# The value products of an image in two visits of two head groups instead of four visits of one

## The reference, cut to what matters

```python
q = (x @ q_w + q_b).reshape(B, N, H, hd).transpose(0, 2, 1, 3)
kv = (cond @ kv_w + kv_b).reshape(B, condN, 2, H, hd)
attn = softmax(einsum('bhnd,bhmd->bhnm', q * scale, k), axis=-1)
out  = einsum('bhnm,bhmd->bhnd', attn, v)          # the value products
x = x + out.transpose(0, 2, 1, 3).reshape(B, N, C) @ proj_w + proj_b
# then: norms, router (softmax, top 2 of 8), two expert layers with silu, weighted sum
```

## Time and profile before

| | |
|---|---|
| median of the runs | 849.52 us |
| span of the profiled execution (first to last instruction) | 811.2 us |
| of it, images in the pipeline (first to last product PV) | 47 to 491 us |
| PE busy | 710.0 us, 88% |
| DVE busy | 613.0 us, 76% |
| ACT busy | 514.1 us, 63% |
| POOL busy | 534.4 us, 66% |
| mean granted PE clock | 0.938 |

### The profile page before, as it was taken

One profiled execution on the slowest core, in us unless ns is written; L12 is line 12 of the kernel. 1 busy time (PEld: TensorE's weight loads), 2 busy tenths in 40 slices (PEclk: granted clock), 3 DMA queues, 4 the chain that ended last, 5 costly groups with the idle time before them and its releaser, 6 DMA issues.

```text
span 811.2 us, 17210 instructions
## 1 busy us (share of the span) xinstructions
PE 710.0 (88%) x5180; PEld 495.4 (61%) x5180; DVE 613.0 (76%) x2106; ACT 514.1 (63%) x1053; POOL 534.4 (66%) x756
## 2 busy tenths in 40 slices
PE   1799999999899989997999987978899999999950
PEld 0565566565565556565566655756688888887740
DVE  3666768978688878787888785677678888889962
ACT  0466666566575766565667656757587777787840
POOL 5522526777687877867688674674367777766672
PEclk9889999899898999899999998989899999999985
DMA  6454536435454455454354427556699887889955
GB/s 187 102 118 134 124 113 142 140 103 165 105 145 138 124 159 133 145 139 140 94 123 102 106 71 250 192 179 218 229 331 309 282 256 248 275 283 360 387 201 175
DMA packets 152292, 146.54 MB, mean 181 GB/s; under 512 B 53403, under 2 KB 108584, under 8 KB 152040
## 3 DMA queue, kind: packets, MB, share of 16 engines
q1 hardware_dynamic: 140808, 121.57, 50.6%
q0 software_dynamic: 9088, 19.68, 7.0%
q10 hardware_dynamic: 2304, 4.20, 1.4%
HBM read 81.56 MB, written 40.86 MB: 151 GB/s over the span
## 4 chain that ended last, share of the span: by engine, by line
PE 59%; DVE 13%; DMA 8%; ACT 6%; issue 6%; SPq 5%; POOL 4%; POOLq 0%; DVEq 0%; ACTq 0%
PE po L656 6%; PE pt L645 6%; SPq L413 5%; DMA qd<-nm 4%; PE ps L632 4%; PE pm L665 3%; PE ps L566 2%; DVE mx L1021 2%; PE ps L568 2%; PE pt L566 2%; PE pm L623 2%; PE pm L750 2%; PE pm L728 2%; PE ps L567 2%; PE pm L752 2%
## 5 line engine op out<-in xcount | busy, mean ns | idle before, releaser
L845 ACT ACTIVATE P<-pt 77x512 f32<-77x512 f32 x256 | 152.1, 595 | 107.2 <-PE pt L645 106.0
L1417 POOL DMA_INDIRECT ys<-yo,to x156 | 161.1, 1033 | 65.2 <-issue 38.9
L1410 POOL DMA_INDIRECT xs<-zz,idx x128 | 132.3, 1034 | 67.2 <-issue 28.3
L1021 DVE TENSOR_REDUCE mx<-ps 128x4 f32<-128x308 f32 x256 | 117.1, 468 | 35.6 <-PE ps L632 34.3
L1280 DVE TENSOR_TENSOR sl<-sf,sh 128x512 fp32r<-128x512 f32 x156 | 107.4, 693 | 47.7 <-ACT sh L898 33.0
L645 PE MATMUL pt<-qd,kc 128*77 128x512 f32 x256 | 115.0, 450 | 13.2 <-DMA qd<-nm 13.1
L656 PE MATMUL po<-P,v 77*9 77x128 f32 x2048 | 106.6, 282 | 0.0
L632 PE MATMUL ps<-kd,qc 128*128 128x308 f32 x256 | 100.5, 395 | 3.6 <-DVE mx L1021 3.2
L1344 POOL TENSOR_SCALAR ve<-mv 128x4 f32<-128x4 f32 x48 | 12.6, 262 | 104.6 <-DVE mv L934 103.0
L896 ACT ACTIVATE sf<-ps 128x512 f32<-128x512 f32 x78 | 46.8, 600 | 49.1 <-PE ps L568 49.1
L632 PEld LDWEIGHTS ps<-kd,qc 128*128 128x128 f32 x256 | 51.0, 200 | 26.6 <-issue 15.2
(11 more groups left out here) (234 smaller groups left out, 1924.1 us busy)
## 6 DMA issues: line engine op xcount, KB each, us to landing
qd<-qc SPq DMA_DIRECT2D x128, 128.0 KB
ws<-wsd SPq DMA_DIRECT2D x26, 512.0 KB, 4.7
w1o<-wsd SPq DMA_DIRECT2D x26, 512.0 KB
w2o<-wsd SPq DMA_DIRECT2D x26, 512.0 KB, 5.0
xb<-xs SPq DMA_DIRECT2D x39, 288.0 KB
kd<-kc SPq DMA_DIRECT2D x128, 77.0 KB, 2.3
wsd<-ws SPq DMA_DIRECT2D x8, 1024.0 KB, 4.3
y<-ys SPq DMA_DIRECT2D x32, 256.0 KB, 6.0
```

Source lines behind the costliest of these rows:

```text
L845: eng.activation(P[k % 4][:, :], pT[k % 2][0:CS, :], ACT.Exp).then_inc(sems["p"], 1)
L1021: eng.tensor_reduce(mx[b % 2][:, 4 * g:4 * g + 4], ps[k % 2][:, 0:KC].rearrange("p (j m) -> p j m", j=4), AX.X, ALU.max, negate=True).then ...
L1410: eng.indirect_dma_start(out=xs, out_offset=at, in_=zz[b][:, j % 4, :], in_offset=None).then_inc(sems[f"sw{b}"], 16)
L1417: eng.indirect_dma_start(out=ys, out_offset=at, in_=yo[u % NYO][:, q, :], in_offset=None).then_inc(sems[f"ys{u % NYO}"], 16)
```

## The change

The string `SLOTS` gets groups joined by a plus sign: Pv2 and Pv3 stand together where Pv2 stood, Pu0 and Pu1 together where Pu0 stood. A joined group counts as one slot, so `near` and `go()` see two slots fewer in each iteration. Nothing is put between the two products of a pair. The buffers of `P` get a name for their number, which stays 4. No product, copy or DMA is added or removed.

```diff
-SLOTS = "SC0 Pv2 ST0 ON SC1 Pv3 ST1 MT SC2 ST2 PR Pu0 OT SC3 ST3 Pu1"
+SLOTS = "SC0 Pv2+Pv3 ST0 ON SC1 ST1 MT SC2 ST2 PR Pu0+Pu1 OT SC3 ST3"
+NP = 4
@@ stage_order
         if t % 2 == 0 and ok(t):
-            steps.append(("QD", t // 2))
+            steps.append([("QD", t // 2)])
...
-        for s in SLOTS.split():
-            name, b = of[s[:2]]
-            if ok(b):
-                steps.append((name, b, int(s[2:])) if s[2:] else (name, b))
+        for slot in SLOTS.split():
+            group = []
+            for s in slot.split("+"):
+                name, b = of[s[:2]]
+                if ok(b):
+                    group.append((name, b, int(s[2:])) if s[2:] else (name, b))
+            if group:
+                steps.append(group)
         n = max(len(steps), 1)
         fed = 0
         for k in range(n):
             if k < len(steps):
-                put(steps[k])
+                for step in steps[k]:
+                    put(step)
@@ tiles
-        P = tile(sa, "P", [CS, 4 * S], F, 4)
+        P = tile(sa, "P", [CS, 4 * S], F, NP)
@@ tensor, PV
-                                     P[k % 4][:, j * S:(j + 1) * S], start=True, stop=True)
+                                     P[k % NP][:, j * S:(j + 1) * S], start=True, stop=True)
@@ scalar, ST
-                w.wait_ge("Og", k - 3)
-                eng.activation(P[k % 4][:, :], pT[k % 2][0:CS, :], ACT.Exp).then_inc(sems["p"], 1)
+                w.wait_ge("Og", k - NP + 1)
+                eng.activation(P[k % NP][:, :], pT[k % 2][0:CS, :], ACT.Exp).then_inc(sems["p"], 1)
```

## The result

The changed kernel takes 862.9 us (median of 4, 860.7 to 865.3) against 848.4 for the kernel before beside it: 2.1% slower, ratio 1.021 (95% interval 1.016 to 1.026). Timed twice more it gave 1.014 (1.008 to 1.021) and 1.017 (1.005 to 1.029). A ratio uses only executions within 1.5% of the fastest of their kernel and a median uses all, so the two can differ a little. The forecast was 834.5 us and faster.

What follows compares the result with a forecast made beforehand. PE's queue was taken to bound the first stage: 37 us gross less returns left 12, raised to 15 for double counting. That took the span from 811.2 to 796.2, plus 38.3 around it: 834.5 us, range 816 to 852.

Steps and rivals of the forecast that it cites:

- What bounds the kernel: First stage: PE's own queue sets the pace, with 6 to 8 us idle in each 100; DVE comes next.
- What a visit costs: Value products on PE: a lone visit costs 0.50 us, a pair 0.76; a pair saves 0.29 us.
- the rival in which a second group doesn't overlap: Pairs on PE: a merge gives only 0.17 us, 22 us gross less 22 of returns; 849 us, chance 0.05.
- Gross gain, 37 us: First stage, PE: 128 merges at 0.29 us each, at the full clock; bounds 31 and 38 us.
- Pv3's wait, 13 us in about 30 places: PE at Pv3 waits for ST3's exponential: loss 0.37 us in 30 images, 0.1 in 16; bounds 0 and 24 us.
- ACT's order, KG iterations, DVE: Returns: ACT's earlier copy of `po` 0.5 us, longer PE waits for KG's evacuation 4.5, queued DVE steps 2.
- The DMAs into `qd`, 3 us: Faster iterations leave the maxima's DMA less time to land before MT; 3 us return, bounds 0 and 11.
- The end of the stage: Fewer go() calls per iteration delay the last router's TP and scatters, so the first block starts later: 2 us, bounds 0 and 3.
- The sum of the returns, 22 us of 37: All waits and delays coming back, less 3 us counted double, leaving a 15 us gain.
- the other engines swallow it: Slack is small in several places, so waits take back the whole PE gain: about 850 us, chance 0.13.
- Slower by the clock: More waits at Pv3 lower the granted clock; doubled low time costs 22 us: 857 us, chance 0.12.
- The second stage keeps its length: Sign of a right forecast: the stage after the last value product, untouched by the change, stays equally long.

Runs made afterwards that it cites:

- second profile: The kernel before, unchanged, run and profiled once more: 848.4 us, span 846.6 us, granted clock 0.929.
- first profile of before: The profile of the unchanged kernel that the prediction read: span 811.2 us, granted clock 0.938.
- first set: Runs beside the unchanged kernel (848.4 us): pairs with empty slots 848.1 us, fewer slots with lone visits 848.8, only Pu0 and Pu1 paired 852.1.
- fourth set: Runs beside the unchanged kernel at 815.0 us: the changed kernel with router steps ahead of RK two slots earlier 811.4; with RK also later 804.2.

## Why the prediction was wrong, by its own steps

- *What bounds the kernel.* Right that PE's queue sets the pace. Wrong in its base: the 38.3 us were taken as lying outside the span. They were two executions of different speed; the low time that I read as some 45 us of the stage was 41 there and 61 in the second profile. This alone doesn't turn the sign, since the sum was a difference.
- *What a visit costs.* Right. A pair takes 0.56 us, and the rival in which a second group doesn't overlap is refuted again by the 16 products in 0.56 above.
- *Gross gain, 37 us.* Of the right order as work taken off PE. Its busy time in the stage fell by 12.0 us while 31 us more were at the low level; at half a microsecond each that is a fall of some 27 (an estimate).
- *Pv3's wait, 13 us in about 30 places.* Measured 9.9 in 25 in the changed kernel, 11.9 in 32 with the old slot count. The size was right there (15.9 in 29 to the end of the stage), its meaning less so: without it the DMA's wait came in its place, and the time didn't fall.
- *ACT's order, KG iterations, DVE.* `kc` 3.3 us against 4.6 in the second profile of before: nothing of the 4.5 came. `mx` isn't among the long waits.
- *The DMAs into `qd`, 3 us.* 12.7 against 10.7, and 12.7 in the first profile of before: the 3 us can't be told from nothing.
- *The end of the stage.* This is the step that failed. I had worked out that `go()` is called 14 or 15 times and not 16 or 17, and followed that to one place only, the last scatters and block 0. The same count shifts norms and router against the images in every group of the stage (13 RKs of the 16 lie in it). RK is the 31st step of its list. With 16 slots in the list's first iteration it stood behind the 15th slot of the next, SC3; with 14 and 15 it stands behind the second slot of the one after, which is the pair Pv2, Pv3, and two slots later it would stand behind ON. Had I walked the list so for one group, I would have found it right behind the wait that I did price. The waits that it brought are 8.8 and 7.8 us, in 12 and 10 places, where before had 1.7 and 0.8. With this step undone and the pairs kept (old slot count) the ratio is 1.000.
- *The sum of the returns, 22 us of 37.* This failed as well, by itself. With the old slot count, where the shift of the router plays no part, the sum would have given 15 us, and the pairs gave none (1.000, 0.995 to 1.005). Of the rivals "the other engines swallow it" (0.13) is what those runs look like. Part of the gain was lost in waits for `qc` (8.4 us against 5.4) and `mx` (3.0 against 2.1) in the first stage, part in a longer second stage; how much each cost wasn't measured.
- *The rivals.* Slower by the clock had a chance of 0.12, a mechanism that fits what the records show, and nearly the right size: I had put the low time at double with 22 us of loss; it went from 61 to 92 us, some 15. It had the wrong place: not at Pv3, where PE waits 0.4 us, but at RK, where it stops about 0.75 us among products that are small themselves. That the time came near its 857 us is in part luck, since its base of 834.5 held a gain that didn't come. The argument against it, that the new waits are short, looked at single waits and not at how thin PE's work around them becomes.
- *The second stage keeps its length.* 339.1 against 344.0 us, with a clock of 0.92 and 0.90. So 4.9 of the 16.8 us that the span grew lie here. It has 70 us at the low level where before had 54; at 0.28 to 0.5 us each that is 4 to 8 us (an estimate), enough for the difference.

With RK out of the way too the pairs aren't shown to be worth anything: 840.3 us with them and 840.0 without, ratios 0.985 (0.978 to 0.993) and 0.991 (0.988 to 0.995). At most they keep some 5 us of the 37.

## What to carry to other kernels

In a kernel with one written order, an edit of the order also moves all that is placed by counting its entries. Walk every list that is paced by the count through a whole period, and look for a step that now comes right behind the one that makes its input; the new stop is often not where the edit is. And when PE's work in a stretch gets thinner, by shorter work or by stops, look at the granted clock of that stretch before counting the saved microseconds: here a better place for four tiny matmuls moved the time by 3% in the changed kernel (0.9% in the kernel before), the pairs by nothing that stands clear of the scatter.

## What the runs showed of the hardware

Value products with 9 array columns cost 0.07 to 0.10 us at each border with wider ones, and two groups of 4 heads in a row take 0.56 us instead of twice 0.33. Over 18 executions of the unchanged kernel in the first set (841 to 853 us) the time goes with the granted clock (0.939 to 0.919), at 0.28 us for each microsecond at the low level by a fitted line; between two profiles of one set with the stage's low time 61 and 65 us apart it was 0.45 to 0.47. In the changed kernel's first profile the 14 spells at the low level in the first stage last 3.4 to 13.7 us each, all of them longer than PE's longest stop for `mcum` in that stage (1.1 us). And the same kernel takes 815.0 us in one set and 846 to 857 in the others, 4 to 5% apart, at nearly the same granted clock (0.930 and 0.937 in the first and fourth set, whose records carry the same chip number, 12); what sets it isn't shown.

The version with the lowest ratio is the change with RK two slots later: 0.983 (0.978 to 0.988) to the kernel before. The pairs with the old slot count and RK later, at 0.985 (0.978 to 0.993), can't be told from it.
